# Graph network kernel on one core: 66 more row gathers and 48 more fp32 products in its setup

## The reference

```python
def _cgconv(x, src, dst, attr, Wf, bf, Ws, bs):
    z = jnp.concatenate([x[dst], x[src], attr], axis=-1)
    m = jax.nn.sigmoid(z @ Wf + bf) * jax.nn.softplus(z @ Ws + bs)
    agg = jax.ops.segment_sum(m, dst, num_segments=N)
    return agg + x
# h = leaky_relu(graph_norm(cgconv(x, ...)))      first layer, table x
# h = leaky_relu(graph_norm(cgconv(h, ...)))      second layer, table h
x = layernorm(x + h)
Wh = x @ W + b                                    # third part, table Wh
sim = cosine(Wh[src], Wh[dst])
prop = segment_sum(base * relu(+-sim) * Wh[dst], src)
x = layernorm(x + scale * (coeff[0] * prop_pos + coeff[1] * prop_neg + coeff[2] * Wh))
```

## Time and profile before

| what | us |
|---|---|
| device time, median of two runs | 11563.73 |
| the two runs | 11554.88 and 11572.58 |
| span of the profiled execution, first to last instruction | 11550.1 |

### The profile page before, as it was taken

The page is one execution under the profiler, slowest core; times in us unless marked ns, Lnnn a source line. Parts: engine busy times, 40 slices in busy tenths (PEclk is TensorE's granted clock), DMA queues, the critical chain, the costliest instruction groups (busy, mean ns, idle before and its releaser), DMA issues. The chain is left out here.

```text
span 11550.1 us, 89590 instructions
## 1 busy us (share of the span) xinstructions
PE 4750.4 (41%) x15982; PEld 2985.0 (26%) x15982; DVE 4365.6 (38%) x7054; ACT 2260.1 (20%) x3460; POOL 7691.0 (67%) x6875
## 2 busy tenths in 40 slices
PE   0067776777206666777641222222222222222221
PEld 0033333333103333333321222222222222222221
DVE  2333333333303333333333344444444444444445
ACT  0033333333103333333321101001001010010100
POOL 5556656555435665666653688888888888888885
PEclk9977778878557777777775555555555555555555
DMA  7233333333203333333320233333333333333333
GB/s 278 66 93 97 96 97 96 96 96 94 89 25 87 93 93 89 93 94 91 93 72 20 32 36 37 36 36 37 36 37 36 36 37 36 37 36 36 37 36 75
DMA packets 869598, 790.23 MB, mean 68 GB/s; under 512 B 483674, under 2 KB 621802, under 8 KB 868298
## 3 DMA queue, kind: packets, MB, share of 16 engines
q0 software_dynamic: 398432, 244.82, 17.4%
q1 hardware_dynamic: 461928, 480.85, 13.7%
q10 hardware_dynamic: 9218, 64.36, 1.4%
HBM read 547.94 MB, written 241.38 MB: 68 GB/s over the span
## 5 line engine op out<-in xcount | busy, mean ns | idle before, releaser
L659 POOL DMA_INDIRECT by_src<-arena,put_idx x1568 | 2483.8, 1584 | 482.0 <-issue 482.0
L583 POOL DMA_INDIRECT G<-h_rows,idx x1568 | 1542.1, 983 | 978.2 <-issue 480.6
L583 POOL DMA_INDIRECT G<-in_x,idx x1470 | 1452.8, 988 | 971.0 <-issue 469.5
L760 PE MATMUL ps_gv<-ident,arena 128*128 128x128 f32 x1568 | 385.4, 427 | 3729.8 <-issue 3709.7
L583 POOL DMA_INDIRECT G<-wh_rows,idx x1568 | 1530.0, 976 | 484.3 <-issue 443.1
L760 PEld LDWEIGHTS ps_gv<-ident,arena 128*128 128x128 f32 x1568 | 307.5, 224 | 3790.6 <-issue 3769.7
L1036 DVE TENSOR_TENSOR_SCAN xd_t<-same,xd_t,ps_inj 128x512 f32<-128x512 bf16 x588 | 751.6, 1278 | 1377.5 <-remote 951.5
L712 PE MATMUL ps_gv<-attr,w_attr 65*128 65x512 f32 x1568 | 1089.0, 832 | 391.0 <-DMA attr<-in_attr_t 361.7
L715 PE MATMUL ps_gv<-arena,w_src 128*128 128x512 f32 x1568 | 1034.6, 797 | 0.0
L1179 DVE TENSOR_SCALAR put_idx<-arena,drop 128x8 int32<-128x8 f32 x196 | 45.5, 232 | 2269.4 <-DMA by_src<-arena,put_idx 2269.4
L1059 DVE TENSOR_SCALAR arena<-ps_gv 128x512 f32<-128x512 f32 x392 | 267.5, 682 | 1624.8 <-remote 1071.3
(11 more groups left out here) (161 smaller groups left out, 7026.5 us busy)
## 6 DMA issues: line engine op xcount, KB each, us to landing
inj<-first_edge_rows SPq DMA_DIRECT2D x588, 256.0 KB
running_sums<-arena SPq DMA_DIRECT2D x392, 256.0 KB
same<-same_dst SPq DMA_DIRECT2D x1176, 64.0 KB
first_edge_rows<-zeros ACTq DMA_DIRECT2D x56, 896.0 KB
attr<-in_attr_t SPq DMA_DIRECT2D x392, 128.0 KB
same_sum<-same_dst SPq DMA_DIRECT2D x784, 64.0 KB
G<-h_rows,idx POOLq DMA_INDIRECT x1568
G<-wh_rows,idx POOLq DMA_INDIRECT x1568
```

What stands on the lines that cost most here:

```text
L583: pool.indirect_dma_start(out_, None, table_in, bass.IndirectOffsetOnAxis(ap=index, axis=0)).then_inc(s, 16)
L659: pool.indirect_dma_start(acc_d[a], bass.IndirectOffsetOnAxis(ap=put_idx[:, buf, k:k + 1], axis=0), put[:, buf, k * D:(k + 1) * D], None, ...
L760: mm = pe.transpose(spread[:, buf, k], src_f[:, buf, k:k + 1].to_broadcast([P, P]), ident[:])
```

## The change

POOL gets 66 gathers from `x` between its last scatter of layer 0 and the gather of `seam_get`: eleven widths (128, 127, 126, 124, 122, 120, 112, 96, 64, 32 and 16 rows), six gathers of each. After the six of a width it waits until all of these have landed and increments a semaphore. PE gets 48 fp32 products of 512 columns before its first instruction of layer 0: 12 on the whole array, 12 with 64 output rows (the two halves of the output in turn), 12 with 64 input rows (the halves in turn, into two banks), 12 with both. DVE sets their two inputs beside its other constants. Nothing reads what these gathers and products write. There are three new tiles and two new semaphores.

```diff
@@ tiles
         seam_row = sb("seam_row", [P, D])
+        again = sb("again", [P, 6 * D])
+        lhs_again = sb("lhs_again", [P, P])
+        rhs_again = sb("rhs_again", [P, COLS])
@@ semaphores
         s_end_rows = sem("end_block_gathered")
+        s_again = sem("rows_gathered_again")
+        s_products = sem("product_inputs_ready")
@@ block.gpsimd
                     pool.wait_ge(s_edges, 16 * 8)
+                    landed = 0
+                    for rows in (P, 127, 126, 124, 122, 120, 112, 96, 64, 32, 16):
+                        for k in range(6):
+                            pool.indirect_dma_start(
+                                again[0:rows, k * D:(k + 1) * D], None, x,
+                                bass.IndirectOffsetOnAxis(ap=src_i[0:rows, k:k + 1], axis=0)).then_inc(s_again, 16)
+                        landed += 16 * 6
+                        pool.wait_ge(s_again, landed)
+                        pool.sem_inc(s_ptick, 1)
@@ block.tensor
             pe.wait_ge(s_weights, 16 * (2 * 19 + 2))
+            pe.wait_ge(s_products, 1)
+            for _ in range(12):
+                pe.matmul(ps_gv[:, 0, 0], lhs_again[:], rhs_again[:], start=True, stop=True)
+            for _ in range(6):
+                for half in range(2):
+                    part = slice(half * D, (half + 1) * D)
+                    pe.matmul(ps_gv[part, 0, 0], lhs_again[:, 0:D], rhs_again[:], start=True, stop=True)
+            for _ in range(6):
+                for half in range(2):
+                    part = slice(half * D, (half + 1) * D)
+                    pe.matmul(ps_gv[:, 0, half], lhs_again[part, :], rhs_again[part, :], start=True, stop=True)
+            for _ in range(6):
+                for half in range(2):
+                    part = slice(half * D, (half + 1) * D)
+                    pe.matmul(ps_gv[part, 0, half], lhs_again[part, 0:D], rhs_again[part, :], start=True, stop=True)
@@ block.vector
             v.memset(ones[:], 1.0)
+            v.memset(lhs_again[:], 0.5)
+            v.memset(rhs_again[:], 0.25).then_inc(s_products, 1)
```

## The result

| | median us | runs |
|---|---|---|
| before | 11563.73 | 11554.88 to 11572.58 |
| changed | 11685.42 | 11679.76 to 11691.07 |

The changed kernel takes 1.0113 times as long (95% interval 1.0085 to 1.0140), 121.7 us more. The profiled execution has a span of 11678.0 us, 127.9 us above the 11550.1 us of the earlier trace rows, and a time of 11679.76 us. The forecast was 11665 us, with a range of 11610 to 11740 us.

What follows compares the result with a forecast made beforehand. POOL's chain from the last scatter through `seam_get` was taken to bound the start of layer 0. Issue 63.0, pauses 16.5 and landings 21.8 us sum to 101.3 us, added to 11563.7 for 11665 us; range 11610 to 11740 us.

Steps and rivals of the forecast that it cites:

- What bounds the kernel and what sets the place's worth: At the join before layer 0: `seam_get` opens a POOL chain without slack, so added POOL work moves all three layers.
- Issue of full gathers: POOL before `seam_get`: 66 gathers at 0.954 us make 63.0 us, plus 16.5 us of 0.30 us pauses within batches.
- Width: New POOL gathers: every width priced as 128 rows, 63.0 us; cost proportional to rows would give 47.7 us.
- the adding scatter's 1.584 us: Upper bound for a new gather's price, from POOL's costliest DMA form: 41.6 us more for all 66.
- Landing: POOL's eleven waits after batches: 1.98 us each, taken from the scatters just before, 21.8 us together.
- The bound from below that came from PE's start: Landing wait of 1.86 us: PE's transpose starts 1.56 us after its gather, plus POOL's 0.30 us; 20.5 us for eleven.
- Products and memsets: PE's 48 products (28 to 87 us) and DVE's two fills (0.65 us) are covered by existing waits: cost nothing.
- Rival 1: Some gather widths use few DMA engines, so landings come later: 4.7 or 14.4 us more, 11670 or 11679 us; chance 0.25.
- Rival 2: Narrow POOL gathers are cheaper, in proportion to rows: sum 86.0 us, time 11650 us; chance 0.17.
- Rival 3: Products leave PE's clock low for layer 0: 240 to 290 us in all, about 11830 us; chance 0.04.
- the prediction's own sign: In POOL's changed profile, a batch of 127 rows longer than that of 128 shows few DMA engines in use.
- the even landing: Main forecast for the new gathers: full price for every width, rows spread evenly over DMA engines, 11665 us; chance 0.50.

Runs made afterwards that it cites:

- all 128: One line changed so that all eleven gather batches have 128 rows: 10700.22 us, ratio 1.0112 against the kernel before on the same chip.
- the other widths: Gather widths replaced by 128, 127, 125, 121, 119, 113, 62, 61, 31, 17, 13: 10737.96 us in one timed run; kernel before on that chip 10584.59 us.

## Why the prediction was right or wrong

**What bounds the kernel and what sets the place's worth: right.** The edit was read as wholly on the path, since `seam_get` opens the chain through SP to the first gather of layer 0. So it was, by the kernels with the gathers alone and the products alone. The chain is the same after (7.44 us from seam gather to first gather, where it was 7.34), and the rest of the span moved by 0.6 us.

**Issue of full gathers: right.** 63.0 us were forecast, 62.8 us measured with all 128; the pauses of 0.30 us between gathers were as forecast too.

**Width: the step that was mis-sized.** The full price was taken for every width, with a proportional price as the lower end. In fact POOL's time is 0.84 us and 13.4 ns for each row of one DMA engine's share. That makes narrow gathers hardly cheaper (112 to 16 rows: 0.93 to 0.84 us, 1.9 us saved on thirty gathers) and three of the others dear: 6 x 1.60 us for 127 rows, 6 x 0.71 for 122 and 6 x 0.34 for 124, together 15.9 us. The term was 63.0 us and measured 77.3. The upper end that the range took for it, the adding scatter's 1.584 us, was no bound for a single gather either: one of 127 rows takes 2.55 us.

**Landing: mis-sized.** 11 x 1.98 = 21.8 us were forecast from the scatters. Ten of the waits were 2.08 to 3.08 us, the one behind 127 rows 4.99 us, together 28.8 us. The bound from below that came from PE's start (1.86 us) lay further off still: POOL's own waits for a read of 128 rows, less its 0.30 us between instructions, end 1.9 to 2.1 us after the gather, where PE started 1.56 us after it. On top comes the pause of 2.45 us inside the batch of 124 rows, 2.15 us more than a plain one.

**Products and memsets: right.** Nothing, by the kernel with the products alone (1.0006). The ends of 28 and 87 us for their length were right bounds: 29 us were measured, so the halves of the split forms do run side by side: their records start in pairs 0.01 us apart, and 12 products take 5.4 us where 12 whole ones take 10.4 us at 0.86 us each.

**Rival 1: its condition holds, its price was incomplete.** It was given a chance of 0.25 and an effect of 4.7 to 14.4 us, all in the landing. The trace shows its condition in the packets of POOL's DMA queue. The first window holds a gather of 128 rows, the second the sixth of 127 rows, the third one of 126 rows:

```profile
DMA packets 32, 0.03 MB, mean 33 GB/s; under 512 B 16, under 2 KB 16, under 8 KB 32
...
DMA packets 144, 0.04 MB, mean 13 GB/s; under 512 B 136, under 2 KB 136, under 8 KB 144
...
DMA packets 32, 0.03 MB, mean 23 GB/s; under 512 B 18, under 2 KB 18, under 8 KB 32
```

By the sizes that the trace holds for these packets, with 128 rows there are 16 of 2048 bytes (eight rows each) and 16 small ones of 4 bytes, the same number as the count that a landing adds to the semaphore. With 127 rows there are 8 large packets, seven of 4096 bytes and one of 3840, 32512 bytes or 127 rows in all; and besides the 16 small ones there are 120 packets of 64 or 60 bytes, eight for each of fifteen engines. With 126 rows there are 14 packets of nine rows and two of 36 bytes. The small ones of one such engine, seven of 64 bytes and one of 60, are 508 bytes, 127 times four. So the data of 127 rows is in one engine's packets, and the other engines get as many small entries as that one has rows. POOL's time grows with just that number. It is no waiting for the transfers: the first gather of the batch starts after all earlier ones have landed, and takes 2.57 us already.

This is what rival 1 left out: the unequal share costs POOL's own time, 9.6 us for 127 rows, three times as much as the later landing of 3.0 us (forecast 2.8; the same wait was 4.52 us with the gathers alone and 4.4 us on average with 127 rows throughout, so 2.1 to 3.0 us later).

The packets carry no engine's name in this trace, so that the data packets of one gather lie on one engine is concluded from their number and sizes, and whether the six gathers of a batch take different engines stays open. The Trainium skill, "DMA: Bandwidth & Descriptors", in the section on why a DMA increments its semaphore by 16, gives by its rule, the largest number up to 16 that divides the leading dimension on both sides, 1, 14, 4, 2 and 15 engines for 127, 126, 124, 122 and 120 rows. The traces agree for these gathers: by the packets of 128, 127 and 126 rows above, and by twenty widths, in which the rows of one engine give POOL's time (the mean of six) to within 0.04 us. Its exception for some direct copies was not tried.

**Rival 2: fell.** Sixteen rows cost 0.84 us where 128 cost 0.95 us.

**Rival 3: fell.** The grant was at its lower level from 292.17 us, behind the burst, until 694.95 us. Layer 0 still had 0.79 on average, 0.80 before, and the rise to the upper level came as it had: at 694.95 us behind a first old instruction at 667.27 us, and before at 568.02 us behind one at 540.22 us, the same distance to 0.1 us. So the lower level that the burst left behind cost nothing: layer 0 of the kernel before began at it too, by its long products at 3.62 us.

**The sum.** 101.3 forecast, 125.1 measured: 14.3 us from POOL's time by width, 7.0 us from landings, 2.2 us from the pause, and 0.3 us of rounding. The time came out 20 us above the forecast and inside the range, which had been widened upward for another reason, the adding scatter's price. So that it lies inside is in part luck. By the prediction's own sign (a batch of 127 rows longer than the one of 128) it is rival 1, given 0.25, whose condition held, and not the even landing that was given 0.50; and neither of its two sums, 11670 and 11679 us, had the term that decided, POOL's own time by width.

## What to carry to other kernels

Before a gather whose number of rows is no multiple of 16 goes on POOL's path, find the largest divisor of that number up to 16: the rows divided by it are what one engine gets, and POOL pays 13.4 ns for each of them. 127 rows cost 2.7 times the POOL time of 128 and land 2 to 3 us later, so pad the index list to a multiple of 16 where the data allows it; splitting it into 112 and 15 rows took 184 us at the join where whole gathers of 127 took 262. Scatters of other widths were not run. And work that another engine does before it is first needed is free only up to that moment: 168 products were hidden, and 600 were not.

## What the runs showed of the hardware

**A burst starts at the lower clock level, and the granted clock of a window can be no record at all.** The first 12 products took 13.04 us, 1.09 us each, where 600 in a row took 0.86 us each. The windows of the changed kernel on both sides of the trace's first clock record, and then on both sides of the rise in layer 0, are:

```profile
259.82:264.87 5.05, 5.05 (x6) 2.15 (x7) 2.34 (x8) 0.00 (x0) 3.13 (x4) 1.00 0.18 52
264.87:272.79 7.92, 7.92 (x19) 3.23 (x17) 0.00 (x0) 0.00 (x0) 5.09 (x6) 1.00 0.32 81
667.20:694.90 27.70, 11.93 (x26) 6.50 (x27) 2.56 (x2) 1.17 (x2) 21.01 (x22) 0.50 0.33 82
694.95:705.10 10.15, 7.33 (x23) 3.32 (x22) 0.00 (x0) 0.00 (x0) 6.67 (x7) 1.00 0.14 26
```

In the first window the records start 0.86 us apart, the price of the 1.2 GHz level (two records make a product), and in the second 0.43 us. Both windows read 1.00, but only the second has a record behind it. In the same way the long products at 3.62 us for four records in the earlier trace rows stand ahead of 568.02 us, where the first record of that trace starts, and those at 1.88 us behind it. So where a trace's clock records begin late, the speed of the products tells the level and the window's grant does not.

**POOL pauses by itself.** In the kernel with 127 rows throughout pauses stand seven gathers apart. If each gather hands an engine one entry for each row of the fullest engine and one for the semaphore, that is 896 of them, and 1024 with the next gather. In layer 1 of the kernel with products only there are thirteen pauses of 2.0 to 2.1 us, from 3092 to 4853 us, each 112 gathers of 128 rows after the last, which is 1008 entries by the same count, and 1017 with the next. Counted from the first new gather, the pause of the changed kernel comes after 1010 entries (1042 with the next) and that of the other widths after 1014 (1026 with the next). That fits a store of some 1015 entries, an estimate from these counts, which POOL lets run empty before it goes on; that it runs empty is argued and not shown. Against so simple a count speak two things. In the kernel with the other widths a second pause would be due before gather 42, which brings the entries since the first pause to 1020, and there is none. And in the kernel with 112 and 15 rows the one pause came after 640 entries. What starts, empties or resets the count was not tried and stays open.

**Chips differ in layers 0 and 1.** Layer 0 of the kernel with products only, on the chip with 10584.59 us, and layer 2 there:

```profile
577.00:2400.00 1823.00, 1526.17 (x4469) 770.04 (x4468) 859.58 (x931) 808.91 (x1116) 1397.44 (x1397) 0.85 0.47 121
5500.00:10400.00 4900.00, 1186.95 (x6196) 1126.81 (x6196) 2044.47 (x3871) 485.55 (x968) 3952.76 (x3091) 0.54 0.30 37
```

It issues 4469 matmul records in 1823 us where the earlier trace rows show 4485 in 2323 us, while layer 2, where POOL is busy for 3953 of 4900 us, goes at one rate on both. The difference of 979 us between the two chips is eight times the effect of this change, so a kernel with work for PE in its loops is to be compared on one chip alone. The cause stays open. The grant there was 0.85 and not 0.80, and PE took 0.34 us a record and not 0.37, which is too little for a rate 1.27 times as high. What does differ is the waits: over 1000 to 2000 us of the kernel before POOL waits 166.9 us for the loads of indices, and over 1000 to 1785 us on the other chip 0.9 us.
